# Row factors in pairs, two groups normalised on GpSimd and side rows scattered earlier, at the end of an attention and expert kernel

## The chip, the cores and the metric

One core of one Trainium2 chip. The metric is the device time of one execution in microseconds (us), the median of the runs shown. TensorE is PE in the profile, VectorE is DVE, ScalarE is ACT, GpSimd is POOL, SyncE is SP.

## What is computed

Input x is 16 x 256 rows of 256 floats. A multi-head attention layer (16 heads of 16) and a layer with 8 experts follow one another, each with a residual sum and a layer norm:

```python
x = layernorm(x + attention(x, w_q, w_k, w_v, w_o))
x = layernorm(x + experts(x, gating_w, w1, b1, w2, b2))
```

In the second, a softmax over 8 gates picks the best two experts of each of the 4,096 tokens; an expert takes at most 1,280 items, in order of tokens, and computes `relu(g @ w1 + b1) @ w2 + b2`, which is added to the token's row with its normed weight. The layer norm at the end is

```python
m = mean(x); v = var(x)
return (x - m) / sqrt(v + 1e-5)
```

## The kernel before, in words

All matrix products are made in float32 by splitting each factor into a high part and a low part (`h_hi`, `h_lo` and so on) and adding three products. ScalarE and VectorE make the parts. After attention, the rows x1 lie in DRAM twice: as the source for the experts, and as `acc_rows`, to which experts add their outputs with a scattering DMA.

The experts' part (`experts`) runs over 8 experts. An expert's 1,280 slots are 5 chunks (c = 0 to 4) of 256 rows, 2 tiles of 128 rows each, gathered by GpSimd's indirect DMAs into `rows[c]`. Layer 1 runs over "super-chunks": chunks 0 and 1, chunk 2 alone, chunks 3 and 4. A super-chunk has units: in a wide one unit u (0 to 7) is one of the 8 slices of 128 hidden features for 512 rows, six matmuls (L1685 to L1687) into one of four banks in turn. ScalarE's relu (L1475) takes a unit from its bank, VectorE splits it (L1551, L1553). TensorE waits for the relu of unit u - 4 before it fills the bank again. Layer 2 makes the chunk's output tiles (L1714 to L1716 for the last expert). The order of all of this is written out by hand in `expert_order`, and each engine runs its own part of that order.

For the last expert the end differs. Its output isn't added in DRAM. SyncE loads all 4,096 rows of `acc_rows` as eight groups of 4 x 128 rows into `acc_sb` (`a` in the code), VectorE takes their statistics (`row_stats`, L1559), GpSimd makes their row factors (`row_factors`), ScalarE normalises them (`normalise`, L1485), SyncE stores them. Rows that the last expert touches are then overwritten: GpSimd gathers the sums so far into `rows[c]` (`gather_sums`, L1377), VectorE adds the share of the last expert (L1568, L1575) and takes statistics, and when all stores have landed (`stored`) GpSimd scatters the finished rows to the output (`put_rows`, L1415).

Chunks 0 and 1 are the "side rows": GpSimd makes their factors (`fix_factors`) and ScalarE normalises them (`fixed_rows`, L1491). Chunks 2, 3 and the two tiles of chunk 4 are the "end parts" 0 to 3: VectorE makes the variance (L1593, L1600), GpSimd the factor by one power instruction (`end_factor`, L1405), VectorE normalises (`end_rows`, L1607). A factor is (variance + eps) to the power -0.5 (L1386), the column of -0.5 coming from `expo`, set by one memset.

Each engine runs its instructions in order, so a wait holds all that stands behind it. SyncE issues the eight stores in order of the groups. Groups 6 and 7 are normalised by ScalarE one tile after each relu of the last super-chunk (`IN_RELU`). Layer 2 of chunks 2 and 3 in the last expert writes to layer 1's banks, so its tiles wait for the relus of units 4, 5, 6 and 7:

```python
elif e == LASTE and c in (2, 3):
    pe.wait_ge(h_done, unit_no(e, len(SUPERS) - 1, 2 * (c - 1) + r + 2, None) + 1)
```

## Time and profile before

| what | value |
|---|---|
| time, median of 3 runs | 820.42 us (818.41 to 821.08) |
| span of the profiled execution | 856.8 us |
| TensorE matmul busy | 784.5 us, 92% |
| VectorE busy | 605.1 us, 71% |
| ScalarE busy | 442.1 us, 52% |
| GpSimd busy | 410.2 us, 48% |

The profile is of one execution; for it only the span from the first to the last instruction is given, and no second time beside it. Shares are of that span. A row of the timeline has an instruction's start, its duration, its engine and line, what it writes and reads, and in brackets the idle time of the engine before it and what ended it.

### The profile page before, as it was taken

To read this page: it belongs to the slowest core of one execution; us is meant where nothing else is said; L and a number is where in the kernel's file an instruction comes from. 1 tells how busy PE (TensorE), PEld (TensorE's weight loads), DVE (VectorE), ACT (ScalarE), POOL (GpSimd) and SP (SyncE) were. 2 spreads that over 40 slices of the span, in tenths; PEclk is the share of its full clock that TensorE was granted. 3 is DMA by queue.
4 is the path that set the end of the run, shared out by engine and by line. 5 is a ranking of instruction groups with operands and counts; after the bars stand their busy time and mean duration, and the time that the engine had idled before them with its cause. 6 is when DMAs were issued, how large, how long until landed. Compare 5 with 4: busy or idle time off the path is not lost.

```text
span 856.8 us, 16628 instructions
## 1 busy us (share of the span) xinstructions
PE 784.5 (92%) x5919; PEld 648.5 (76%) x5919; DVE 605.1 (71%) x1325; ACT 442.1 (52%) x753; POOL 410.2 (48%) x595
## 2 busy tenths in 40 slices
PE   7699989999989985896999999999999999999994
PEld 7577766677667653585889898898898888988993
DVE  5768878888888885683756856756657568665983
ACT  3166757777666664542534534534345345443670
POOL 1011245555555546457146445254364462556675
PEclk9799999999999998799899999999999999999998
DMA  5677765555555572326145245253352451533741
GB/s 158 135 165 161 161 153 113 114 113 114 116 114 110 115 141 73 116 51 180 20 91 109 41 89 115 43 130 50 81 111 40 96 112 31 140 57 57 288 179 46
DMA packets 71534, 92.75 MB, mean 108 GB/s; under 512 B 12972, under 2 KB 55885, under 8 KB 71324
## 3 DMA queue, kind: packets, MB, share of 16 engines
q1 hardware_dynamic: 53308, 67.95, 31.0%
q0 software_dynamic: 16928, 22.15, 14.9%
q10 hardware_dynamic: 1216, 1.57, 0.8%
q8 instruction: 48, 0.79, 0.4%
q14 instruction: 34, 0.28, 0.1%
HBM read 39.18 MB, written 26.89 MB: 77 GB/s over the span
## 4 chain that ended last, share of the span: by engine, by line
PE 69%; DVE 14%; issue 5%; POOL 3%; another core or an unknown queue 3%; DMA 2%; ACT 2%; ACTq 1%; POOLq 0%; DVEq 0%; SPq 0%
PE bank L1718 14%; DVE negm L890 10%; PE wide L1687 8%; PE wide L1685 8%; PE wide L1686 8%; PE bank L985 7%; PE bank L1720 7%; PE wide L1030 5%; PE bank L1664 2%; PE wide L1048 2%; PE bank L1095 2%; PE bank L1064 1%; PE bank L994 1%; POOL slot_list L533 1%
## 5 line engine op out<-in xcount | busy, mean ns | idle before, releaser
L1359 POOL DMA_INDIRECT acc_rows<-o_w,lists x70 | 120.4, 1720 | 181.6 <-ACT o_w L1508 167.9
L890 DVE TENSOR_REDUCE negm<-wide 128x4 f32<-128x1024 f32 x128 | 156.1, 1222 | 50.5 <-PE wide L1030 31.7
L630 ACT ACTIVATE probs<-wide 128x1024 f32<-128x1024 f32 x128 | 131.0, 1024 | 89.1 <-PE wide L1048 68.9
L1475 ACT ACTIVATE h<-wide,b1T 128x512 f32<-128x512 f32 (+1 forms) x200 | 115.0, 600 | 96.8 <-PE wide L1687 69.1
L1720 PE MATMUL bank<-stack,h_lo 128*128 128x256 f32 x560 | 156.9, 280 | 0.0
L1685 PE MATMUL wide<-g_hi,stack 128*128 128x512 f32 (+1 forms) x400 | 140.8, 352 | 5.2 <-DVE g_lo L1536 4.1
L1687 PE MATMUL wide<-g_hi,stack 128*128 128x512 f32 (+1 forms) x400 | 140.1, 350 | 0.1
L1686 PE MATMUL wide<-g_lo,stack 128*128 128x512 f32 (+1 forms) x400 | 140.1, 350 | 0.0
L1508 ACT ACTIVATE o_w<-o_b,lists 128x256 f32<-128x256 f32 x70 | 35.7, 510 | 148.6 <-DVE o_b L1646 135.5
L1718 PE MATMUL bank<-stack,h_hi 128*128 128x512 f32 x304 | 108.7, 401 | 1.3 <-DVE o_b L1646 1.3
L1720 PEld LDWEIGHTS bank<-stack,h_lo 128*128 128x128 f32 x560 | 105.6, 189 | 0.0
L1348 POOL DMA_INDIRECT rows<-x_rows,lists x80 | 84.3, 1054 | 29.5 <-issue 23.9
L1718 PE MATMUL bank<-stack 128*128 128x512 f32 x256 | 90.4, 396 | 0.0
L1685 PEld LDWEIGHTS wide<-g_hi,stack 128*128 128x128 f32 x400 | 75.9, 190 | 16.4 <-DVE g_lo L1536 4.4
L1030 PE MATMUL wide<-stack 48*128 48x256 f32 x512 | 65.5, 335 | 24.8 <-DVE negm L890 21.2
L1030 PEld LDWEIGHTS wide<-stack 48*128 48x128 f32 x512 | 40.2, 191 | 62.0 <-DVE negm L890 28.7
L1644 DVE TENSOR_TENSOR low<-bank,b_all 128x256 f32<-128x256 f32 x70 | 29.6, 422 | 81.4 <-PE bank L1720 69.4
L1687 PEld LDWEIGHTS wide<-g_hi,stack 128*128 128x128 f32 x400 | 75.9, 190 | 10.6 <-issue 0.3
L1686 PEld LDWEIGHTS wide<-g_lo,stack 128*128 128x128 f32 x400 | 76.0, 190 | 9.7
L1064 PE MATMUL bank<-probs,v_aug 128*32 128x256 f32 x1024 | 72.4, 402 | 9.3 <-ACT probs L630 9.3
L543 POOL CAST xT_hi<-xT_f 128x512 fp32r<-128x512 f32 x14 | 8.5, 610 | 148.3 <-ACT xT_f L585 148.3
L533 POOL DMA_INDIRECT slot_list<-item,dest x64 | 65.5, 1023 | 25.7 <-issue 23.6
(211 smaller groups left out, 1640.9 us busy)
## 6 DMA issues: line engine op xcount, KB each, us to landing
stack<-qk SPq DMA_DIRECT2D x180, 128.0 KB, 4.2
...
```

Source lines behind the costliest of these rows:

```text
L630: nc.scalar.activation(probs[:, i % 4].rearrange("p x c t -> p x (c t)"), shifted_banks(i)[:, :, :], ACT.Exp, scale=SCALE).then_inc(exp_do ...
L890: nc.vector.tensor_reduce(negm[n % 2][:, :, :, u].rearrange("p c x -> p x c"), score_banks(PAIRS * n + u)[:, :, :].rearrange("p x (c t) -> ...
L1030: ins = nc.tensor.matmul(out[:, x, c * S:c * S + S], st[k, u, 0, c * P:c * P + P], st[k, u, 1, :], start=True, stop=True, tile_position=(H ...
L1064: ins = nc.tensor.matmul(out, v_aug[n % VB][:, c, 4 * t + j, :], probs[:, u % 4, j % 2, c, :], start=(c == 0), stop=(c == QC - 1), tile_po ...
L1348: nc.gpsimd.indirect_dma_start(out=rows[c][:, r, :], out_offset=None, in_=x1_d, in_offset=bass.IndirectOffsetOnAxis(ap=lists[:, e, QC * c ...
L1359: nc.gpsimd.indirect_dma_start(out=acc_d, out_offset=bass.IndirectOffsetOnAxis(ap=lists[:, e, QC * c + r, 0:1], axis=0), in_=o_w[c][:, r, ...
L1475: ins = nc.scalar.activation(h[u % 2][:, t], banks[BZ[u % 4]][:, t], ACT.Relu, bias=b1T[:, FT * e + f:FT * e + f + 1])
L1685: nc.tensor.matmul(out, w1_hi[:, k, fs], g_hi[i % 2][:, k, cols], start=(k == 0), stop=False)
L1686: nc.tensor.matmul(out, w1_hi[:, k, fs], g_lo[i % 2][:, k, cols], start=False, stop=False)
L1687: ins = nc.tensor.matmul(out, w1_lo[:, k, fs], g_hi[i % 2][:, k, cols], start=False, stop=(k == DK - 1))
L1718: nc.tensor.matmul(banks[BO[r]], H_hi[:, f, rs], w2_both[:, f, :, :].rearrange("p x d -> p (x d)"), start=(f == 0), stop=False)
L1720: ins = nc.tensor.matmul(out_half(r, 1), H_lo[:, f, rs], w2_hi[:, f, :], start=False, stop=(f == FT - 1))
```

## The change

- `expo` grows from 4 to 8 columns.
- `row_factors` takes two groups in one set of four instructions, on 8 columns instead of 4; there are four sets where there were eight.
- GpSimd's order: the factors of groups 0 and 1, then the gathers of chunks 3 and 4 (which stood behind all factors), then the factors of groups 2 to 7.
- Groups 6 and 7 are normalised by GpSimd (`last_groups`), four tiles each, as (row - mean) x factor; they count on `own_done`, for which SyncE now waits ahead of these two stores.
- `fix_factors` makes the factors of both side chunks at once.
- The side rows' four tiles are normalised by ScalarE one after each relu of units 4 to 7 (`SIDE_UNIT`), where it had the tiles of groups 6 and 7 after all eight; before, the side rows came after the last relu.
- The four scatters of the side rows all stand before the factor of end part 0, where one stood before and three after it.

```diff
@@ -88,7 +88,7 @@
         b1T = sb("b1T", [P, NE * FT])
         w1_raw = sb("w1_raw", [P, DK, FF])
         w2_raw = sb("w2_raw", [P, FT, D])
-        expo = sb("expo", [P, 2 * QC])
+        expo = sb("expo", [P, 4 * QC])
         w1_loaded, w2_loaded, b2_loaded = sem("w1_loaded"), sem("w2_loaded"), sem("b2_loaded")
         w1_hi_done, w1_lo_done, w2_hi_done, w2_lo_done = sem("w1_hi_done"), sem("w1_lo_done"), sem("w2_hi_done"), sem("w2_lo_done")
         list0_loaded, list1_loaded, lists_loaded, late0_loaded, late_loaded = (
@@ -1203,8 +1203,9 @@
     LASTE, LASTC = NE - 1, NC - 1
     PAIR = 2
     FIRST_STATS = 2
-    IN_RELU = (6, 7)
+    OWN = (6, 7)
     SIDE = 2
+    SIDE_UNIT = 4
     LAST_BANKS = ((4, 5), (6, 7), (0, 1), (2, 3), (4, 5))
     acc_v = acc_d[0:T, :].rearrange("(g p t) d -> g p t d", p=P, t=GROUP)
     out_rows = out_d.rearrange("b s d -> (b s) d")
@@ -1253,7 +1254,7 @@
         acc_loaded = [sem(f"acc_loaded{i}") for i in range(NG)]
         stats_done, norm_parts, rstd_done, shift_done, out_done, stored = (sem(n) for n in (
             "stats2_done", "norm_parts2", "rstd2_done", "shift2_done", "out_done", "out_stored"))
-        low_done = sem("low_done")
+        low_done, own_done = sem("low_done"), sem("own_done")
         fix_stats = sb("fix_stats_sb", [P, NC, QC, 3])
         fix_veps, fix_nmean, fix_rstd, fix_shift = (sb(n, [P, NC, QC]) for n in ("fix_veps", "fix_nmean", "fix_rstd", "fix_shift"))
         end_stats = sb("end_stats", [P, QC, 6])
@@ -1332,7 +1333,10 @@
             for i in range(NG):
                 sp.dma_start(a[:, i], acc_v[i]).then_inc(acc_loaded[i], 16)
             for i in range(NG):
-                sp.wait_ge(out_done, GROUP * (i + 1))
+                if i in OWN:
+                    sp.wait_ge(own_done, GROUP * (i - OWN[0] + 1))
+                else:
+                    sp.wait_ge(out_done, GROUP * (i + 1))
                 sp.dma_start(out_v[i], a[:, i]).then_inc(stored, 16)
             sp.wait_ge(stored, 16 * NG)
             for c in range(NC):
@@ -1378,26 +1382,36 @@
                         out=rows[c][:, r, :], out_offset=None, in_=acc_d,
                         in_offset=bass.IndirectOffsetOnAxis(ap=lists[:, LASTE, QC * c + r, 0:1], axis=0)).then_inc(gathered[c], 16)
 
-            def row_factors(i):
...
+            def row_factors(b):
+                two = slice(2 * b, 2 * b + 2)
+                pool.wait_ge(stats_done, GROUP // PAIR * (2 * b + 2))
+                nc.gpsimd.tensor_scalar(veps[:, two, :], stats[:, two, :, 2], 1.0 / D, EPS, ALU.mult, ALU.add).then_inc(norm_parts, 1)
+                nc.gpsimd.tensor_scalar(nmean[:, two, :], stats[:, two, :, 1], -1.0, None, ALU.mult).then_inc(norm_parts, 1)
+                pool.wait_ge(norm_parts, 2 * b + 1)
+                nc.gpsimd.tensor_tensor(rstd[:, two, :], veps[:, two, :], minus_half[:, :].rearrange("p (i t) -> p i t", i=2),
+                                        ALU.pow).then_inc(rstd_done, 1)
+                pool.wait_ge(norm_parts, 2 * b + 2)
+                pool.wait_ge(rstd_done, b + 1)
+                nc.gpsimd.tensor_tensor(shift[:, two, :], nmean[:, two, :], rstd[:, two, :], ALU.mult).then_inc(shift_done, 1)
+
+            def last_groups():
+                pool.wait_ge(rstd_done, NG // 2)
+                for i in OWN:
+                    for t in range(GROUP):
+                        nc.gpsimd.tensor_scalar(a[:, i, t, :], a[:, i, t, :], stats[:, i, t, 1:2], rstd[:, i, t:t + 1],
+                                                ALU.subtract, ALU.mult).then_inc(own_done, 1)
+
+            def fix_factors():
+                side = slice(0, SIDE)
+                pool.wait_ge(fix_stats_done, SIDE)
+                nc.gpsimd.tensor_scalar(fix_veps[:, side, :], fix_stats[:, side, :, 2], 1.0 / D, EPS, ALU.mult, ALU.add).then_inc(norm_parts, 1)
+                nc.gpsimd.tensor_scalar(fix_nmean[:, side, :], fix_stats[:, side, :, 1], -1.0, None, ALU.mult).then_inc(norm_parts, 1)
+                pool.wait_ge(norm_parts, NG + 1)
+                nc.gpsimd.tensor_tensor(fix_rstd[:, side, :], fix_veps[:, side, :],
+                                        minus_half[:, 0:SIDE * QC].rearrange("p (c r) -> p c r", c=SIDE), ALU.pow).then_inc(rstd_done, 1)
+                pool.wait_ge(norm_parts, NG + 2)
+                pool.wait_ge(rstd_done, NG // 2 + 1)
+                nc.gpsimd.tensor_tensor(fix_shift[:, side, :], fix_nmean[:, side, :], fix_rstd[:, side, :], ALU.mult).then_inc(shift_done, 1)
 
             def end_factor(j):
                 c, cols = END_PARTS[j]
@@ -1409,7 +1423,7 @@
 
                 for r in tiles:
                     if c < SIDE:
-                        pool.wait_ge(out_done, GROUP * NG + QC * c + r + 1)
+                        pool.wait_ge(out_done, GROUP * OWN[0] + QC * c + r + 1)
                     else:
                         pool.wait_ge(fix_out_done, QC * (c - SIDE) + r + 1)
                     nc.gpsimd.indirect_dma_start(
@@ -1422,19 +1436,17 @@
                 add_back(n // NC, n % NC)
             for c in range(3):
                 gather_sums(c)
-            for i in range(FIRST_STATS):
-                row_factors(i)
-            for i in range(FIRST_STATS, NG):
-                row_factors(i)
+            row_factors(0)
             gather_sums(3)
             gather_sums(4)
+            for b in range(1, NG // 2):
+                row_factors(b)
+            last_groups()
+            fix_factors()
+            pool.wait_ge(stored, 16 * NG)
             for c in range(SIDE):
-                fix_factors(c)
-            pool.wait_ge(stored, 16 * NG)
-            put_rows(0, (0,))
+                put_rows(c)
             end_factor(0)
-            put_rows(0, (1,))
-            put_rows(1)
             put_rows(2)
             end_factor(1)
             put_rows(3)
@@ -1475,31 +1487,26 @@
                         ins = nc.scalar.activation(h[u % 2][:, t], banks[BZ[u % 4]][:, t], ACT.Relu,
                                                    bias=b1T[:, FT * e + f:FT * e + f + 1])
                     ins.then_inc(h_done, 1)
-                    if e == LASTE and s == len(SUPERS) - 1:
-                        i, t = divmod(u, GROUP)
-                        normalise(IN_RELU[i], (t,))
-
-            def normalise(i, tiles=range(GROUP)):
-                act.wait_ge(shift_done, i + 1)
-                for t in tiles:
+                    if e == LASTE and s == len(SUPERS) - 1 and u >= SIDE_UNIT:
+                        fixed_row(*divmod(u - SIDE_UNIT, QC))
+
+            def normalise(i):
+                act.wait_ge(shift_done, i // 2 + 1)
+                for t in range(GROUP):
                     nc.scalar.activation(a[:, i, t, :], a[:, i, t, :], ACT.Identity, bias=shift[:, i, t:t + 1],
                                          scale=rstd[:, i, t:t + 1]).then_inc(out_done, 1)
 
-            def fixed_rows(c):
-                act.wait_ge(shift_done, NG + c + 1)
-                for r in range(QC):
-                    nc.scalar.activation(rows[c][:, r, :], rows[c][:, r, :], ACT.Identity, bias=fix_shift[:, c, r:r + 1],
-                                         scale=fix_rstd[:, c, r:r + 1]).then_inc(out_done, 1)
+            def fixed_row(c, r):
+                act.wait_ge(shift_done, NG // 2 + 1)
+                nc.scalar.activation(rows[c][:, r, :], rows[c][:, r, :], ACT.Identity, bias=fix_shift[:, c, r:r + 1],
+                                     scale=fix_rstd[:, c, r:r + 1]).then_inc(out_done, 1)
 
             def weigh(e, c, tiles=range(QC)):
                 n = NC * e + c
                 if e == LASTE:
                     if c == 0:
-                        for i in range(IN_RELU[0]):
+                        for i in range(OWN[0]):
                             normalise(i)
-                    if c == 2:
-                        for i in range(SIDE):
-                            fixed_rows(i)
                     return
                 if e > 0:
                     act.wait_ge(added[c], 16 * QC * e)
@@ -1601,7 +1608,7 @@
 
             def end_rows(j):
                 c, cols = END_PARTS[j]
-                dve.wait_ge(rstd_done, NG + SIDE + j + 1)
+                dve.wait_ge(rstd_done, NG // 2 + 1 + j + 1)
                 for r in range(cols.start, cols.stop):
                     mean = fix_stats[:, c, r, 1:2] if c < LASTC else end_mv[:, r, 0:1]
                     nc.vector.tensor_scalar(rows[c][:, r, :], rows[c][:, r, :], mean, fix_rstd[:, c, r:r + 1],
```

GpSimd from the last three rows of the first gathers on, before:

```order
L1377 DMA rows<-acc_rows,lists 128x256 [waits added2,added3,added1,added4,added0,gT_ready]
L1377 DMA rows<-acc_rows,lists 128x256
L1383 TENSOR_SCALAR veps<-stats 128x4 [waits stats2_done]
L1384 TENSOR_SCALAR nmean<-stats 128x4
L1386 TENSOR_TENSOR rstd<-veps,expo 128x4 [waits norm_parts2]
L1389 TENSOR_TENSOR shift<-nmean,rstd 128x4 [waits rstd2_done,norm_parts2]
L1383 TENSOR_SCALAR veps<-stats 128x4 [waits stats2_done]
L1384 TENSOR_SCALAR nmean<-stats 128x4
L1386 TENSOR_TENSOR rstd<-veps,expo 128x4 [waits norm_parts2]
L1389 TENSOR_TENSOR shift<-nmean,rstd 128x4 [waits rstd2_done,norm_parts2]
L1383 TENSOR_SCALAR veps<-stats 128x4 [waits stats2_done]
L1384 TENSOR_SCALAR nmean<-stats 128x4
L1386 TENSOR_TENSOR rstd<-veps,expo 128x4 [waits norm_parts2]
L1389 TENSOR_TENSOR shift<-nmean,rstd 128x4 [waits rstd2_done,norm_parts2]
```

and now:

```order
L1381 DMA rows<-acc_rows,lists 128x256 [waits added2,added3,added1,added4,added0,gT_ready]
L1381 DMA rows<-acc_rows,lists 128x256
L1388 TENSOR_SCALAR veps<-stats 128x8 [waits stats2_done]
L1389 TENSOR_SCALAR nmean<-stats 128x8
L1391 TENSOR_TENSOR rstd<-veps,expo 128x8 [waits norm_parts2]
L1395 TENSOR_TENSOR shift<-nmean,rstd 128x8 [waits rstd2_done,norm_parts2]
L1381 DMA rows<-acc_rows,lists 128x256 [waits added2,added3,added1,added4,added0,gT_ready]
L1381 DMA rows<-acc_rows,lists 128x256
L1381 DMA rows<-acc_rows,lists 128x256 [waits added2,added3,added1,added4,added0,gT_ready]
L1381 DMA rows<-acc_rows,lists 128x256
L1388 TENSOR_SCALAR veps<-stats 128x8 [waits stats2_done]
L1389 TENSOR_SCALAR nmean<-stats 128x8
L1391 TENSOR_TENSOR rstd<-veps,expo 128x8 [waits norm_parts2]
L1395 TENSOR_TENSOR shift<-nmean,rstd 128x8 [waits rstd2_done,norm_parts2]
L1388 TENSOR_SCALAR veps<-stats 128x8 [waits stats2_done]
L1389 TENSOR_SCALAR nmean<-stats 128x8
L1391 TENSOR_TENSOR rstd<-veps,expo 128x8 [waits norm_parts2]
L1395 TENSOR_TENSOR shift<-nmean,rstd 128x8 [waits rstd2_done,norm_parts2]
L1388 TENSOR_SCALAR veps<-stats 128x8 [waits stats2_done]
L1389 TENSOR_SCALAR nmean<-stats 128x8
L1391 TENSOR_TENSOR rstd<-veps,expo 128x8 [waits norm_parts2]
L1395 TENSOR_TENSOR shift<-nmean,rstd 128x8 [waits rstd2_done,norm_parts2]
L1401 TENSOR_SCALAR acc_sb<-acc_sb,stats,rstd 128x256 [waits rstd2_done]
L1401 TENSOR_SCALAR acc_sb<-acc_sb,stats,rstd 128x256 x7
L1407 TENSOR_SCALAR fix_veps<-fix_stats_sb 128x4 [waits fix_stats_done]
```

The factors of groups 2 to 7 have gone behind the gathers of chunks 3 and 4, three sets of four instructions instead of six, and the eight tiles of `acc_sb` stand between the last of them and the side factors.

GpSimd at its end, before:

```order
L1415 DMA out<-rows,lists 4096x256 [waits out_done,out_stored]
L1405 TENSOR_TENSOR fix_rstd<-fix_veps,expo 128x2 [waits end_steps]
L1415 DMA out<-rows,lists 4096x256 [waits out_done] x3
L1415 DMA out<-rows,lists 4096x256 [waits fix_out_done] x2
L1405 TENSOR_TENSOR fix_rstd<-fix_veps,expo 128x2 [waits end_steps]
L1415 DMA out<-rows,lists 4096x256 [waits fix_out_done] x2
L1405 TENSOR_TENSOR fix_rstd<-fix_veps,expo 128x1 [waits end_steps]
L1415 DMA out<-rows,lists 4096x256 [waits fix_out_done]
L1405 TENSOR_TENSOR fix_rstd<-fix_veps,expo 128x1 [waits end_steps]
L1415 DMA out<-rows,lists 4096x256 [waits fix_out_done]
```

and now:

```order
L1414 TENSOR_TENSOR fix_shift<-fix_nmean,fix_rstd 128x4 [waits rstd2_done,norm_parts2]
L1429 DMA out<-rows,lists 4096x256 [waits out_done,out_stored]
L1429 DMA out<-rows,lists 4096x256 [waits out_done] x3
L1419 TENSOR_TENSOR fix_rstd<-fix_veps,expo 128x2 [waits end_steps]
L1429 DMA out<-rows,lists 4096x256 [waits fix_out_done] x2
L1419 TENSOR_TENSOR fix_rstd<-fix_veps,expo 128x2 [waits end_steps]
L1429 DMA out<-rows,lists 4096x256 [waits fix_out_done] x2
L1419 TENSOR_TENSOR fix_rstd<-fix_veps,expo 128x1 [waits end_steps]
L1429 DMA out<-rows,lists 4096x256 [waits fix_out_done]
L1419 TENSOR_TENSOR fix_rstd<-fix_veps,expo 128x1 [waits end_steps]
L1429 DMA out<-rows,lists 4096x256 [waits fix_out_done]
```

The three scatters of side rows that stood behind the first factor of an end part (L1405, now L1419) now stand ahead of it.

ScalarE at its end now, from the last normalised group on (the relus are L1487):

```order
L1496 ACTIVATE acc_sb<-acc_sb,shift,rstd 128x256 [waits shift2_done]
L1496 ACTIVATE acc_sb<-acc_sb,shift,rstd 128x256 x3
L1487 ACTIVATE h<-wide,b1T 128x512 [waits h_lo_done,z_ready,h_hi_done] x5
L1501 ACTIVATE rows<-rows,fix_shift,fix_rstd 128x256 [waits shift2_done]
L1487 ACTIVATE h<-wide,b1T 128x512 [waits h_lo_done,z_ready,h_hi_done]
L1501 ACTIVATE rows<-rows,fix_shift,fix_rstd 128x256 [waits shift2_done]
L1487 ACTIVATE h<-wide,b1T 128x512 [waits h_lo_done,z_ready,h_hi_done]
L1501 ACTIVATE rows<-rows,fix_shift,fix_rstd 128x256 [waits shift2_done]
L1487 ACTIVATE h<-wide,b1T 128x512 [waits h_lo_done,z_ready,h_hi_done]
L1501 ACTIVATE rows<-rows,fix_shift,fix_rstd 128x256 [waits shift2_done]
```

Before, each of the eight relus had one tile of `acc_sb` behind it, and the four tiles of side rows stood after the last.

## Rows read from the trace of the kernel before

**Rows 1.** The page: the chain that ended last, shares by engine.

```profile
PE 69%; DVE 14%; issue 5%; POOL 3%; another core or an unknown queue 3%; DMA 2%; ACT 2%; ACTq 1%; POOLq 0%; DVEq 0%; SPq 0%
```

**Rows 2.** Two stretches: busy us (x instructions) by engine, TensorE's clock, DMA.

```profile
806.00:840.00 34.00, 34.00 (x242) 31.90 (x241) 29.62 (x59) 23.71 (x46) 25.94 (x46) 1.00 0.49 187
840.00:850.00 10.00, 4.05 (x34) 3.84 (x33) 3.81 (x12) 0.00 (x0) 6.43 (x8) 0.93 0.16 54
```

**Rows 3.** Timeline of GpSimd in the tail.

```profile
834.27 0.88 POOL L1405 TENSOR_TENSOR fix_rstd<-fix_veps,expo 128x2 f32<-128x2 f32 x1 [0.78 <-DVE fix_veps L1593]
...
840.80 0.97 POOL L1415 DMA_INDIRECT out<-rows,lists  x1 [0.30 <-issue]
841.78 0.74 POOL L1405 TENSOR_TENSOR fix_rstd<-fix_veps,expo 128x2 f32<-128x2 f32 x1
843.78 1.04 POOL L1415 DMA_INDIRECT out<-rows,lists  x1 [1.26 <-DVE rows L1607]
...
846.11 0.60 POOL L1405 TENSOR_TENSOR fix_rstd<-fix_veps,expo 128x1 f32<-128x1 f32 x1
...
850.87 1.04 POOL L1415 DMA_INDIRECT out<-rows,lists  x1 [1.26 <-DVE rows L1607]
```

**Rows 4.** Timeline of VectorE: splits of the last super-chunk, then the tail.

```profile
820.56 0.40 DVE L1551 CAST stack<-h 128x512 fp32r<-128x512 f32 x1
...
828.84 0.69 DVE L1553 TENSOR_TENSOR h_lo<-h,stack 128x512 fp32r<-128x512 f32 x1
...
839.73 0.17 DVE L1593 TENSOR_SCALAR fix_veps<-fix_stats_sb 128x2 f32<-128x2 f32 x1
...
842.56 0.74 DVE L1607 TENSOR_SCALAR rows<-rows,fix_stats_sb,fix_rstd 128x256 f32<-128x256 f32 x2 [2.66 <-POOL fix_rstd L1405]
...
847.06 0.48 DVE L1575 SCALAR_TENSOR_TENSOR rows<-bank,lists,rows 128x256 f32<-128x256 f32 x1
```

**Rows 5.** Timeline of TensorE: first matmul of unit 4, of layer 2, and the last.

```profile
821.12 0.39 PE L1685 MATMUL wide<-g_hi,stack 128*128 128x512 f32 x1
...
826.69 0.28 PE L1714 MATMUL wide<-stack,h_hi 128*128 128x256 f32 x1
...
843.77 0.28 PE L1716 MATMUL bank<-stack,h_lo 128*128 128x256 f32 x1
```

**Rows 6.** Timeline of ScalarE: groups 0 to 5, then the first relu.

```profile
806.67 4.05 ACT L1485 ACTIVATE acc_sb<-acc_sb,shift,rstd 128x256 f32<-128x256 f32 x8
811.56 6.02 ACT L1485 ACTIVATE acc_sb<-acc_sb,shift,rstd 128x256 f32<-128x256 f32 x12 [0.84 <-POOL shift L1389]
817.79 2.08 ACT L1485 ACTIVATE acc_sb<-acc_sb,shift,rstd 128x256 f32<-128x256 f32 x4 [0.21 <-POOL shift L1389]
819.77 0.67 ACT L1475 ACTIVATE h<-wide,b1T 128x512 f32<-128x512 f32 x1
```

**Rows 7.** Timeline of GpSimd: factors, gathers, and one disturbed instruction.

```profile
803.80 1.18 POOL L1386 TENSOR_TENSOR rstd<-veps,expo 128x4 f32<-128x4 f32 x1
...
811.61 0.20 POOL L1383 TENSOR_SCALAR veps<-stats 128x4 f32<-128x4 f32 x1
...
812.08 1.04 POOL L1386 TENSOR_TENSOR rstd<-veps,expo 128x4 f32<-128x4 f32 x1
813.26 0.20 POOL L1389 TENSOR_TENSOR shift<-nmean,rstd 128x4 f32<-128x4 f32 x1
...
822.44 1.26 POOL L1377 DMA_INDIRECT rows<-acc_rows,lists  x1 [0.69 <-issue]
...
826.55 0.95 POOL L1377 DMA_INDIRECT rows<-acc_rows,lists  x1 [0.30 <-issue]
...
827.86 0.98 POOL L1395 TENSOR_SCALAR fix_nmean<-fix_stats_sb 128x2 f32<-128x2 f32 x1
```

**Rows 8.** Groups of GpSimd by shape: busy, mean ns, idle before.

```profile
L547 POOL TENSOR_TENSOR xT_lo<-xT_f,xT_hi 128x512 fp32r<-128x512 f32 x14 | 17.9, 1279 | 1.2
...
L543 POOL CAST xT_hi<-xT_f 128x512 fp32r<-128x512 f32 x14 | 8.5, 610 | 148.3 <-ACT xT_f L585 148.3
```

More of the change, by code:

```diff
@@ L1379, in gather_sums @@
                         in_offset=bass.IndirectOffsetOnAxis(ap=lists[:, LASTE, QC * c + r, 0:1], axis=0)).then_inc(gathered[c], 16)
-            def row_factors(i):
-                pool.wait_ge(stats_done, GROUP // PAIR * (i + 1))
-                nc.gpsimd.tensor_scalar(veps[:, i, :], stats[:, i, :, 2], 1.0 / D, EPS, ALU.mult, ALU.add).then_inc(norm_parts, 1)
-                nc.gpsimd.tensor_scalar(nmean[:, i, :], stats[:, i, :, 1], -1.0, None, ALU.mult).then_inc(norm_parts, 1)
-                pool.wait_ge(norm_parts, 2 * i + 1)
-                nc.gpsimd.tensor_tensor(rstd[:, i, :], veps[:, i, :], minus_half[:, :], ALU.pow).then_inc(rstd_done, 1)
-                pool.wait_ge(norm_parts, 2 * i + 2)
-                pool.wait_ge(rstd_done, i + 1)
-                nc.gpsimd.tensor_tensor(shift[:, i, :], nmean[:, i, :], rstd[:, i, :], ALU.mult).then_inc(shift_done, 1)
@@ L1391, in fix_factors @@
-            def fix_factors(c):
-                j = NG + c
-                pool.wait_ge(fix_stats_done, c + 1)
-                nc.gpsimd.tensor_scalar(fix_veps[:, c, :], fix_stats[:, c, :, 2], 1.0 / D, EPS, ALU.mult, ALU.add).then_inc(norm_parts, 1)
-                nc.gpsimd.tensor_scalar(fix_nmean[:, c, :], fix_stats[:, c, :, 1], -1.0, None, ALU.mult).then_inc(norm_parts, 1)
-                pool.wait_ge(norm_parts, 2 * j + 1)
-                nc.gpsimd.tensor_tensor(fix_rstd[:, c, :], fix_veps[:, c, :], minus_half[:, 0:QC], ALU.pow).then_inc(rstd_done, 1)
-                pool.wait_ge(norm_parts, 2 * j + 2)
-                pool.wait_ge(rstd_done, j + 1)
-                nc.gpsimd.tensor_tensor(fix_shift[:, c, :], fix_nmean[:, c, :], fix_rstd[:, c, :], ALU.mult).then_inc(shift_done, 1)
+            def row_factors(b):
[9 more added lines that the diff above has]
+                nc.gpsimd.tensor_tensor(shift[:, two, :], nmean[:, two, :], rstd[:, two, :], ALU.mult).then_inc(shift_done, 1)
```

## The prediction

> **What bounds the kernel now.** I read the page first: TensorE is the largest share of the chain that ended last, but VectorE (14%) and GpSimd (3%) stand on it too, and the change touches only the end [rows 1]. So I read the end by stages: TensorE is busy without a gap to 840 and stops inside 840 to 845, yet the span goes on to 856.8 [rows 2]. Two parts of the end decide, and everything below is told in the times of that one execution.
>
> *The tail, from 832 on.* GpSimd's rows show scatter DMAs (L1415) one each 1.27 us (0.97 and 0.30 of issue), of the four side tiles and of chunk 2's two, the last starting at 840.80, and the row factor of chunk 3 (L1405) only behind them at 841.78 [rows 3]. What it needs, the variance of chunk 3, was ready at 839.73 + 0.17 = 839.90 [rows 4]: so GpSimd's queue was late by 841.78 - 839.95 = 1.83 us. From there the work alternates: factor, VectorE normalises (L1607, it waited 2.66 us for the factor), scatter, next factor. The last scatter starts at 850.87, 9.09 us after 841.78 [rows 3, 4]. TensorE was done at 843.77 + 0.28 = 844.05 [rows 5], before VectorE asked for its last sum at 847.06 [rows 4]. The tail is bound by GpSimd's order, not by TensorE.
>
> *The stage before, 806 to 828.* ScalarE normalises groups 0 to 5 (8 + 12 + 4 instructions, 0.50 us each), then starts the relu of unit 0 of the last super-chunk at 819.77, done at 820.44 [rows 6]. TensorE starts unit 4 (which takes unit 0's bank) at 821.12, with no gap [rows 5]. So ScalarE has 0.68 us to spare, and beyond that each us that it is late holds TensorE, and with it everything behind.
>
> **The change part by part.**
>
> 1. *Side rows ahead.* The four scatters of chunks 0 and 1 now stand before the factor of chunk 2. If they are issued before chunk 2's variance is there (the factor starts at 834.27, released by it [rows 3]), only chunk 2's own two are left before chunk 3's factor. Chunk 2's scatters then run 836.9 to 839.2 (VectorE's first row of chunk 2 at about 836.1, plus 0.81, the distance from a normalised tile at 842.97 to the scatter at 843.78; then 1.27 and 0.97 [rows 3, 4]). Chunk 3's factor starts at 839.95 as soon as its variance is there, and the 9.09 us behind it are the same instructions as before. TensorE's 844.05 still comes before VectorE's last sum (845.2). **Tail: -1.83 us.**
>
> 2. *Factors for two groups at once, and the gathers of chunks 3 and 4 (four DMAs) moved ahead of groups 2 to 7.* The power instruction costs 0.60, 0.74 and 1.04 us for 1, 2 and 4 columns [rows 3, 7], some 0.15 a column, so I take 1.64 for 8: 0.6 more than one of 4. The trace has none of 8. From below it is 1.04 (nothing more than for 4), from above 2.08 (twice that); I take the line through the three rows. For groups 0 and 1: power at 803.80 now 1.18 + 0.6, shift done at 806.0; ScalarE asks at 806.67, so it costs nothing there [rows 6, 7]. Next stand the gathers: 0.69 of issue and 5.06 us for four (822.44 to 827.50) [rows 7], so 806.0 to 811.8. They don't wait: chunks 3 and 4 are transposed by then, since ScalarE converts them before it turns to the groups at 806.67 [rows 6]. Then groups 2 and 3: a group took 1.85 us (811.61 to 813.26 + 0.20) [rows 7], two now 2.45, done at 814.3. Before, ScalarE had group 2 at 811.56 [rows 6]. **ScalarE starts group 2 some 2.7 us later.** Groups 4 and 5 are ready at 816.9 and no longer in the way. 16 instructions (12 took 6.02, 4 took 2.08) end at 814.3 + 8.05 = 822.35, the relu of unit 0 starts 0.1 before that as it did before, ends at 822.9, and TensorE takes unit 4 at 823.05, the 0.12 between them being what lay between that relu's end and VectorE's split at 820.56 [rows 4]. Against 821.12 that is a hold of **+1.92 us**. With the bounds of the power (it counts twice, -0.6 or +0.44 each) the hold is 0.7 to 2.8 us. Nothing takes it back: TensorE has no gap from there to its end [rows 2]. All times of the tail move with it, and part 1's gain stays what it is.
>
> 3. *GpSimd normalises groups 6 and 7.* Eight instructions leave ScalarE's relus, eight of 128x256 come to GpSimd. For units 0 to 3 ScalarE has nothing between relus; they are held by VectorE's splits, so it gains nothing on TensorE. On GpSimd the nearest rows are the one-input cast of 128x512 (0.61) and the two-input subtract of 128x512 (1.28) [rows 8]; half of each is 0.31 and 0.64, and the bounds are 0.31 and the whole 1.28. I take p = 0.5, near the cast, as there is one tensor read. Factors of groups 6 and 7 end at 819.4, the eight at 823.4, the side factors (four columns: 1.85 as for a group, and 0.6 if VectorE disturbs them as it did the instruction at 827.86 [rows 7]) at 825.9. ScalarE wants them after the relu of unit 4, about 827.0 (relus keep pace with VectorE's splits, 0.40 + 0.69 a unit [rows 4], from 823.05): covered by 1.1 us. If p grows, the cover is gone at 0.64, but TensorE feels it only when the relu of unit 5 is later than 831.5, where layer 2 of chunk 2, second tile, waits for it (layer 2 began at 826.69 and made six tiles by 843.9, 2.87 each [rows 5]: 826.69 + 1.92 + 2.87); that needs the side shift by 830.3, so p up to about **1.07**. Behind a late shift stand on ScalarE the relus of units 5, 6 and 7. Cost: 0.
>
> 4. *Stores and scatters.* SyncE now waits for group 5 at 822.4 and group 7 at 823.4, where before group 7's last tile stood behind the last relu; so the wait for all stores that stands ahead of the scatters ends earlier. The scatters follow the four side rows (827.5 to 830.7) with 0.8 us and end at about 833.1; chunk 2's factor could start at 834.27 + 1.92 = 836.2. Slack 3 us: cost 0. The queues' earlier gathers meet loads that are nearly over; VectorE's statistics hide them, so I give that nothing. Fewer GpSimd instructions (18 less) count only in the times above.
>
> **Sum:** -1.83 + 1.92 = +0.1 us, so the span 856.8 becomes 856.9. The profiled execution's span stands 36.4 us above the median of the runs shown (820.42), and no row says where; I carry the difference over in full: **820.5 us**. About 0.3% (2.5 us) is what a measurement of this kernel can tell from no change.
>
> **Rivals.**
>
> *The gain alone.* If 8 columns cost the power what 4 do, and ScalarE runs a little tighter, the hold is 0.7 or less and the result lies between -1.1 and -1.83: 818.6 to 819.3. For it: TensorE's slack of 0.68 us, and timed runs that are 4% shorter than this trace, so that the gathers may be too. Against it: the four gathers alone delay group 2 by more than the slack. Chance 0.23.
>
> *GpSimd too slow for the eight tiles, so that the relus stall.* Place: the side shift on ScalarE between the relus of units 4 and 5. It decides from p = 1.07, and each us of p above costs 8 us. At p = 1.28 it is 8 x 0.21 = +1.7 (822.2). While VectorE ran its casts and two-input subtracts, GpSimd's tensor-scalar on two columns took 0.98, against 0.20 for one on four columns undisturbed [rows 7]; if each of the eight also waits for one VectorE subtract of 0.69 [rows 4], p = 1.28 + 0.69 = 1.97 and it costs +7.2 (827.7). For it: those rows, and no row of this instruction. Against it: VectorE has little to do from 820.6 to 823.0, when most of the eight run, and its statistics before that left GpSimd undisturbed (0.20, while they ran). Chance 0.14. The Trainium skill, SBUF — State Buffer, section "SBUF: two separate sides", says that VectorE in a two-port mode or with two SBUF inputs and GpSimd take a shared port pair as an exclusive lock, and the loser blocks for the whole instruction. By that rule alone, 0.69 on each of the eight, p is 1.19 and the sum 1.0 us more, 821.5; the 0.98 agrees with it, the 0.20 says that it doesn't always strike.
>
> *The side rows don't get out of the way.* If stores or side rows come so late that their scatters still stand before chunk 3's factor, the gain is lost and the hold stays: 820.4 + 1.9 = 822.3. It would need the side rows 6 us later than I have them. Chance 0.06.
>
> **How the numbers follow.** My case has 0.57, the rivals 0.23, 0.14 and 0.06. My case with its bounds spans 819.3 to 821.4; the first rival reaches down to 818.6, the third and the lower part of the second up to 822.3. With the scatter of the medians (818.41 to 821.08) the range is 818.4 to 822.7, which leaves out the dear half of the second rival and the best luck. Faster by over 0.3% takes the first rival and some 0.7 us more: 0.12. Slower by over 0.3% takes the second rival with p above 1.38, or the third and some luck: 0.16. Within: 0.72.
>
> **What would show it.** In the profile after: chunk 3's factor directly behind its variance, with GpSimd idle before it, and the last scatter 9.1 us later; side scatters done before chunk 2's factor. A gap of near 1.9 us on TensorE before unit 4, released by the relu, and ScalarE's group 2 starting near 814.3. The power on 8 columns near 1.64. The eight tiles on GpSimd near 0.5. Wrong it would be if that gap on TensorE is under 0.7, if the power isn't in the 1.04 to 2.08, or if ScalarE waits for the side shift by more than 3 us.

## The result, and the profile after

| kernel | median us (range, runs) | ratio to before, 95% interval |
|---|---|---|
| before | 820.84 (818.41 to 821.79, 7) | |
| changed | 823.95 (821.89 to 826.25, 7) | 1.0036 [1.0022, 1.0051] |

The change made the kernel 3.1 us slower. The forecast was 820.5 us with a range to 822.7.

The profiled execution of the changed kernel has a span of 822.4 us in a run of 824.11 us, so some 1.7 us lie around the span. The profile before (856.8) was held up far ahead of the end, in places that the change doesn't touch. Matched instruction by instruction on TensorE, it falls behind the profile after by some 16 us up to 329, by 13 more up to 365 (in the stretch 330 to 350 TensorE's clock was 0.83 and 0.50, and TensorE was busy 2.43 us of the first ten) and by the rest up to 444; from there to the last super-chunk the distance stays at 37.5. What held it up is not shown. So spans aren't compared; the end is, from TensorE's first matmul of the last super-chunk to the start of the last scatter. That is 850.87 - 815.55 = 35.32 us before and 816.46 - 778.02 = 38.44 us after: **3.12 us more**, all of the difference (3.1 us) between the medians. What stood at 815.55 before stands 37.5 earlier now.

TensorE's timeline, its first matmul of the last super-chunk and the two that waited in the end:

```profile
778.02 0.39 PE L1692 MATMUL wide<-g_hi,stack 128*128 128x512 f32 x1
...
785.70 0.50 PE L1692 MATMUL wide<-g_hi,stack 128*128 128x512 f32 x1 [1.94 <-ACT h L1487]
...
795.94 0.39 PE L1721 MATMUL wide<-stack,h_hi 128*128 128x256 f32 x1 [1.54 <-ACT h L1487]
```

The first gap is the hold that was forecast, in its place, at unit 4: [rows 5] had none. From the first matmul of unit 0 to that of unit 4 it is 785.70 - 778.02 = 7.68 us, and 821.12 - 815.55 = 5.57 before: a hold of 2.11, where 1.92 was forecast (the 1.94 in the row is idle time alone). The second, 1.54 us at the second tile of chunk 2, was part of a rival. ScalarE shows what made both:

```profile
777.09 7.99 ACT L1496 ACTIVATE acc_sb<-acc_sb,shift,rstd 128x256 f32<-128x256 f32 x16 [3.68 <-POOL shift L1395]
784.99 1.24 ACT L1487 ACTIVATE h<-wide,b1T 128x512 f32<-128x512 f32 x2
...
794.72 0.60 ACT L1501 ACTIVATE rows<-rows,fix_shift,fix_rstd 128x256 f32<-128x256 f32 x1 [3.97 <-POOL fix_shift L1414]
795.22 0.67 ACT L1487 ACTIVATE h<-wide,b1T 128x512 f32<-128x512 f32 x1
```

Groups 2 to 5 begin 3.68 us after ScalarE was free, and [rows 6] answers to that with 0.84. The side rows (L1501) waited 3.97 us for GpSimd's side shift, with the relu of unit 5 behind them. GpSimd, from the power on eight columns on:

```profile
775.02 1.69 POOL L1391 TENSOR_TENSOR rstd<-veps,expo 128x8 f32<-128x8 f32 x1
...
782.22 10.51 POOL L1401 TENSOR_SCALAR acc_sb<-acc_sb,stats,rstd 128x256 f32<-128x256 f32 x8
...
794.48 0.20 POOL L1414 TENSOR_TENSOR fix_shift<-fix_nmean,fix_rstd 128x4 f32<-128x4 f32 x1
796.26 1.11 POOL L1429 DMA_INDIRECT out<-rows,lists  x1 [1.57 <-DMA out<-acc_sb]
...
800.23 1.09 POOL L1429 DMA_INDIRECT out<-rows,lists  x1 [0.30 <-issue]
802.42 0.88 POOL L1419 TENSOR_TENSOR fix_rstd<-fix_veps,expo 128x2 f32<-128x2 f32 x1 [1.10 <-DVE fix_veps L1600]
...
807.37 0.74 POOL L1419 TENSOR_TENSOR fix_rstd<-fix_veps,expo 128x2 f32<-128x2 f32 x1
...
816.46 1.04 POOL L1429 DMA_INDIRECT out<-rows,lists  x1 [1.26 <-DVE rows L1614]
```

The eight tiles of groups 6 and 7 (L1401) take 782.22 to 792.8, 1.32 us each on average: the first three, before VectorE's splits, 1.22 from start to start, the other five 1.39. So the side shift is there only at 794.68. The side scatters are out of the way before chunk 2's factor (802.42), but that factor comes 24.4 us after the super-chunk's start, where it came 834.27 - 815.55 = 18.7 after it in [rows 3]. VectorE lies between the side shift and that factor:

```profile
785.68 0.48 DVE L1558 CAST stack<-h 128x512 fp32r<-128x512 f32 x1 [2.52 <-ACT h L1487]
786.20 0.93 DVE L1560 TENSOR_TENSOR h_lo<-h,stack 128x512 fp32r<-128x512 f32 x1
...
795.92 0.43 DVE L1558 CAST stack<-h 128x512 fp32r<-128x512 f32 x1 [3.33 <-ACT h L1487]
...
798.93 0.75 DVE L1560 TENSOR_TENSOR h_lo<-h,stack 128x512 fp32r<-128x512 f32 x1
...
802.17 0.17 DVE L1600 TENSOR_SCALAR fix_veps<-fix_stats_sb 128x2 f32<-128x2 f32 x1
...
806.25 0.17 DVE L1600 TENSOR_SCALAR fix_veps<-fix_stats_sb 128x2 f32<-128x2 f32 x1
...
808.15 0.73 DVE L1614 TENSOR_SCALAR rows<-rows,fix_stats_sb,fix_rstd 128x256 f32<-128x256 f32 x2 [1.73 <-POOL fix_rstd L1419]
```

It splits units 5 to 7 only from 795.92 on, then takes the sums and the variance of chunk 2 (802.17). [rows 4] had the splits of a unit at 0.40 and 0.69, here 0.48 and 0.93 while GpSimd's tiles ran. Chunk 3's variance was ready at 806.42, and its factor came at 807.37, behind the second scatter of chunk 2: still 0.95 us late. So the forecast sign of a factor directly behind its variance did not show in this kernel.

### The profile page after: what moved, and what is told of

The parts are those of the page before. It is cut to its first block, busy times and chain, and to the rows that moved or that the text cites. A ratio compares the mean times of both kernels' runs of the same rounds, so it can differ in the third digit from the quotient of the medians.

```text
span 822.4 us, 16603 instructions
## 1 busy us (share of the span) xinstructions
PE 772.8 (94%) x5919; PEld 643.3 (78%) x5919; DVE 606.3 (74%) x1325; ACT 438.8 (53%) x745; POOL 411.7 (50%) x583
## 3 DMA queue, kind: packets, MB, share of 16 engines
q10 hardware_dynamic: 1216, 1.57, 0.9%
## 4 chain that ended last, share of the span: by engine, by line
PE 69%; DVE 13%; POOL 8%; issue 5%; DMA 3%; ACT 1%; ACTq 1%; POOLq 0%; SPq 0%; DVEq 0%
PE bank L1725 14%; PE bank L985 11%; DVE negm L890 9%; PE wide L1694 7%; PE wide L1693 7%; PE wide L1692 7%; PE bank L1727 7%; PE wide L1030 7%; PE wide L1048 2%; PE bank L994 2%; PE bank L1671 2%; PE bank L1095 1%; POOL acc_sb L1401 1%; POOL slot_list L533 1%; DMA acc_rows<-o_w,lists 1%
## 5 line engine op out<-in xcount | busy, mean ns | idle before, releaser
L1487 ACT ACTIVATE h<-wide,b1T 128x512 f32<-128x512 f32 (+1 forms) x200 | 115.2, 601 | 92.6 <-PE wide L1694 66.5
L1515 ACT ACTIVATE o_w<-o_b,lists 128x256 f32<-128x256 f32 x70 | 35.7, 510 | 148.3 <-DVE o_b L1653 148.3
L1692 PEld LDWEIGHTS wide<-g_hi,stack 128*128 128x128 f32 x400 | 75.4, 189 | 13.9 <-ACT h L1487 3.2
L1064 PE MATMUL bank<-probs,v_aug 128*32 128x256 f32 x1024 | 68.5, 385 | 1.0 <-ACT probs L630 1.0
```

What stands on the lines that cost most here:

```text
L1487: ins = nc.scalar.activation(h[u % 2][:, t], banks[BZ[u % 4]][:, t], ACT.Relu, bias=b1T[:, FT * e + f:FT * e + f + 1])
L1692: nc.tensor.matmul(out, w1_hi[:, k, fs], g_hi[i % 2][:, k, cols], start=(k == 0), stop=False)
```

## The experiments

Each was run beside the kernel before. "End" is the stretch defined above, in the profile of each, less the 35.32 us of before.

| label | what | ratio, 95% interval | end, us |
|---|---|---|---|
| changed | | 1.0036 [1.0022, 1.0051] | +3.12 |
| e1_small_tiles | tiles of 8 columns | 1.0005 [0.9994, 1.0016] | +0.39 |
| e2_small_late_gathers | and gathers behind the factors | 1.0024 [1.0011, 1.0037] | +2.32 |
| e3_factors_first | side factors ahead of the tiles | 1.0057 [1.0036, 1.0078] | +5.08 |
| e4_tiles_on_vector | tiles on VectorE | 1.0004 [0.9993, 1.0014] | +0.16 |
| e5_forms | other forms among the eight | one run | +0.75 |
| e9_columns | fewer columns in three of the eight | one run | +0.96 |
| e6_small_gathers_last | e1, gathers behind side factors | 0.9985 [0.9975, 0.9995] | -0.90 |
| e7_vector_one_group | whole, rearranged | 0.9984 [0.9970, 0.9998] | -1.70 |
| e8_and_factors_early | e7, and the last factors earlier | 0.9957 [0.9943, 0.9971] | -2.66 |

**e1_small_tiles.** The price of the tiles taken away, their place kept.

```diff
-    nc.gpsimd.tensor_scalar(a[:, i, t, :], a[:, i, t, :], stats[:, i, t, 1:2], rstd[:, i, t:t + 1],
+    nc.gpsimd.tensor_scalar(a[:, i, t, 0:8], a[:, i, t, 0:8], stats[:, i, t, 1:2], rstd[:, i, t:t + 1],
```

> The changed kernel, but GpSimd's eight instructions on groups 6 and 7 take 8 of 256 columns (the other 248 columns of those tiles are left out of the normalisation). Theory A (the price p = 1.37 us of these eight is what made the change slower): ScalarE gets the side shift about 9.4 us earlier and no longer waits for it, TensorE's second gap (1.5 us at layer 2 of chunk 2) is gone, the first (1.9 us at unit 4) stays, chunk 3's factor stands directly behind its variance; 0.1 us above the kernel before, ratio 1.000. Rival B (the new order of the side scatters and the gathers is slow by itself): still 3 us slower, ratio 1.004.

It came as theory A had it, 1.0005. GpSimd's timeline:

```profile
780.59 3.07 POOL L1401 TENSOR_SCALAR acc_sb<-acc_sb,stats,rstd 128x8 f32<-128x8 f32 x8
...
785.75 0.60 POOL L1414 TENSOR_TENSOR fix_shift<-fix_nmean,fix_rstd 128x4 f32<-128x4 f32 x1
...
797.31 0.89 POOL L1419 TENSOR_TENSOR fix_rstd<-fix_veps,expo 128x2 f32<-128x2 f32 x1 [1.96 <-DVE fix_veps L1600]
...
803.03 0.72 POOL L1419 TENSOR_TENSOR fix_rstd<-fix_veps,expo 128x2 f32<-128x2 f32 x1 [0.79 <-DVE fix_veps L1600]
...
812.10 1.04 POOL L1429 DMA_INDIRECT out<-rows,lists  x1 [1.25 <-DVE rows L1614]
```

The side shift comes at 786.35, and chunk 3's factor (803.03) follows a wait for its variance, not a scatter. TensorE's waits in this stretch (us, times, longest):

```profile
PE wide L1692 <- ACT h L1487: 1.9, 1, 1.9
```

That is one wait, the first. So all but 0.4 us of the loss hung on the price of the eight tiles; what is left is hold less gain, 2.11 less 1.7, forecast at +0.1.

**e2_small_late_gathers.** Meant to take away TensorE's first gap.

```diff
-            row_factors(0)
+            for b in range(NG // 2):
+                row_factors(b)
             gather_sums(3)
             gather_sums(4)
-            for b in range(1, NG // 2):
-                row_factors(b)
```

> As the kernel with small tiles (248 columns of each tile of groups 6 and 7 are left out of the normalisation), and the gathers of chunks 3 and 4 behind all four sets of row factors instead of behind the first. Theory A: ScalarE has group 2 some 2.5 us earlier, TensorE's gap at unit 4 is gone, the tail keeps its 1.8 us: 1.8 us faster than the kernel before, ratio 0.998. Rival C (TensorE's gap at unit 4 doesn't matter, since the tail is bound by GpSimd's chain): the same time as with small tiles alone.

Both missed: 1.0024. The first gap shrank to 0.7, but the four gathers now stood ahead of the tiles and the side factors. GpSimd's tiles of 8 columns and ScalarE's first side row:

```profile
786.86 4.87 POOL L1401 TENSOR_SCALAR acc_sb<-acc_sb,stats,rstd 128x8 f32<-128x8 f32 x8
```

```profile
793.74 0.60 ACT L1500 ACTIVATE rows<-rows,fix_shift,fix_rstd 128x256 f32<-128x256 f32 x1 [5.03 <-POOL fix_shift L1414]
```

ScalarE waited 5.03 us, and the old stall was back by another way. It tells something all the same: from the side shift to the last scatter it is 815.59 - 793.70 = 21.9 us here and 816.46 - 794.68 = 21.8 in the changed kernel. Once the side shift is late, the end hangs on it alone in these two traces, whatever gap TensorE had at unit 4 (0.66 here, 1.94 in the changed kernel).

**e3_factors_first.** Does only ScalarE's wait cost?

```diff
-            last_groups()
             fix_factors()
+            last_groups()
```

> The changed kernel with the side factors ahead of the eight tiles on GpSimd. Theory A: ScalarE no longer waits for the side shift and TensorE's second gap is gone, but the eight tiles (11 us) end 2.9 us later, the last store lands later, and the four side scatters (5 us) start only behind it and stand in front of chunk 2's factor: chunk 3's factor is late again, some 1 us later than in the changed kernel; 4 us above the kernel before, ratio 1.005. Rival D (only the wait of ScalarE costs): as the kernel before, ratio 1.000.

Theory A holds (1.0057), D doesn't. TensorE's second gap is gone, but the last store is later:

```profile
785.89 11.25 POOL L1401 TENSOR_SCALAR acc_sb<-acc_sb,stats,rstd 128x256 f32<-128x256 f32 x8
800.66 1.11 POOL L1429 DMA_INDIRECT out<-rows,lists  x1 [3.52 <-DMA out<-acc_sb]
...
805.79 0.74 POOL L1419 TENSOR_TENSOR fix_rstd<-fix_veps,expo 128x2 f32<-128x2 f32 x1
...
819.21 1.04 POOL L1429 DMA_INDIRECT out<-rows,lists  x1 [1.26 <-DVE rows L1614]
```

The tiles end at 797.1 and the side scatters wait 3.52 us for the store behind them, then stand in front of chunk 2's factor.

**e4_tiles_on_vector.** The same eight tiles, whole, on VectorE behind the side sums.

```diff
+            def last_groups():
+                dve.wait_ge(rstd_done, NG // 2)
+                for i in OWN:
+                    for t in range(GROUP):
+                        nc.vector.tensor_scalar(a[:, i, t, :], a[:, i, t, :], stats[:, i, t, 1:2], rstd[:, i, t:t + 1],
+                                                ALU.subtract, ALU.mult).then_inc(own_done, 1)
...
                         fixed_sums(i)
+                    last_groups()
```

> The changed kernel with the eight tiles of groups 6 and 7 on VectorE, behind the sums of the side rows, where the changed kernel's trace has VectorE idle for 2.5 us. At 0.37 us a tile (two took 0.73 at the end) they are 2.9 us, so the split of unit 0 is 0.4 us late and nothing waits for it. Theory A: no wait for the side shift, one gap of 1.9 us on TensorE; 0.1 to 0.5 us above the kernel before, ratio 1.000 to 1.001. Rival B: still 3 us slower.

1.0004, as theory A. VectorE's row of the eight:

```profile
782.02 2.65 DVE L1613 TENSOR_SCALAR acc_sb<-acc_sb,stats,rstd 128x256 f32<-128x256 f32 x8
```

0.33 us a tile where GpSimd took 1.22 to 1.39; the first split came at 784.60, after which nothing was late.

**e5_forms and e9_columns.** The price itself, in one run each. In e5 the eight have different forms (two constants; one operation with the mean; a copy; 128 and 64 columns; a product); in e9 the first three have 128, 64 and 8 columns and the fourth is one operation with a constant:

```diff
+                        cols = {0: 128, 1: 64, 2: 8}.get(k, D)
+                        at = a[:, i, t, 0:cols]
+                        if k == 3:
+                            ins = nc.gpsimd.tensor_scalar(at, at, 0.5, None, ALU.subtract)
+                        else:
+                            ins = nc.gpsimd.tensor_scalar(at, at, m, r, ALU.subtract, ALU.mult)
```

> The changed kernel with five different instructions among the eight of GpSimd on groups 6 and 7 (the values of those two groups aren't normalised as they should be): in order, the form as it was; two constants instead of the mean and the factor of the row; one operation with the row's mean; a copy; the form as it was on 128 columns and on 64 columns; a product of the tile with itself; the form as it was. This measures the price by form. Theory E (the two values per row, read from memory, make it dear): constants 0.45 us, one operation with the mean about 0.8, 128 and 64 columns 0.8 and 0.5, copy 0.4, product 0.75, whole form 1.25 to 1.38. Theory F (two operations make it dear, whatever the operands): constants 1.2, one operation 0.7.

> The changed kernel with other instructions among GpSimd's eight on groups 6 and 7 (whose values aren't normalised as they should be): first the form as it was on 128, 64 and 8 columns, then one operation with a constant on 256, then four as they were. The first four run before VectorE's splits begin, so this gives the price by columns undisturbed; in the kernel with five forms the 128 and the 64 columns (1.06 and 0.91 us) ran beside VectorE's splits. Theory H (a fixed part of 0.35 us and 3.5 ns a column): 128 columns 0.80, 64 columns 0.57, 8 columns 0.38. Theory I (the fixed part is 0.8 us or more): 128 and 64 columns as before, 1.06 and 0.91. One operation with a constant: 0.7 to 0.93.

GpSimd's groups by form in e5 (busy, mean ns), then rows of its timeline in e9:

```profile
L1417 POOL TENSOR_SCALAR acc_sb<-acc_sb,stats,rstd 128x256 f32<-128x256 f32 x2 | 2.6, 1316 | 0.0
L1405 POOL TENSOR_SCALAR acc_sb<-acc_sb 128x256 f32<-128x256 f32 x1 | 1.1, 1077 | 0.0
...
L1407 POOL TENSOR_SCALAR acc_sb<-acc_sb,stats 128x256 f32<-128x256 f32 x1 | 0.9, 925 | 0.0
...
L1409 POOL CAST acc_sb<-acc_sb 128x256 fp32r<-128x256 f32 x1 | 0.4, 397 | 0.0
```

```profile
782.09 0.81 POOL L1409 TENSOR_SCALAR acc_sb<-acc_sb,stats,rstd 128x128 f32<-128x128 f32 x1
...
783.45 0.40 POOL L1409 TENSOR_SCALAR acc_sb<-acc_sb,stats,rstd 128x8 f32<-128x8 f32 x1
783.83 0.87 POOL L1407 TENSOR_SCALAR acc_sb<-acc_sb 128x256 f32<-128x256 f32 x1
784.67 1.23 POOL L1409 TENSOR_SCALAR acc_sb<-acc_sb,stats,rstd 128x256 f32<-128x256 f32 x1
...
787.25 1.38 POOL L1409 TENSOR_SCALAR acc_sb<-acc_sb,stats,rstd 128x256 f32<-128x256 f32 x1
```

Undisturbed, the form with mean and factor costs 0.40 on 8 columns, 0.81 on 128 and 1.23 on 256: a fixed 0.38 us and 3.3 ns a column, close to theory H (0.35 and 3.5). Neither E nor F holds alone: two constants still cost 1.08, one constant 0.87, one operation with the mean 0.93, and a copy 0.40. The largest step, 0.47, lies between the copy (in e5 a cast to another float32 form) and one operation with a constant; a second operation adds 0.21, and reading the row's two values 0.15. The Trainium skill, GPSIMD Engine Reference, section "4.1 Engine selection", has GpSimd about twice as slow as VectorE for two inputs and calls one input roughly line-rate. VectorE took 0.33 for the whole form, so the copy's 0.40 is near that, and the tensor-scalar's 0.87 to 1.23 on the same 256 columns is not.

e5 and e9 show one thing more. Their eight instructions are cheaper together, and TensorE had a single gap again, the one at unit 4; ScalarE still waited 1.86 us for the side shift. From e5, TensorE's waits in the end, then GpSimd, ScalarE and the last scatter:

```profile
PE wide L1708 <- ACT h L1503: 1.8, 1, 1.8
```

```profile
793.41 0.20 POOL L1430 TENSOR_TENSOR fix_shift<-fix_nmean,fix_rstd 128x4 f32<-128x4 f32 x1
793.65 0.60 ACT L1517 ACTIVATE rows<-rows,fix_shift,fix_rstd 128x256 f32<-128x256 f32 x1 [1.86 <-POOL fix_shift L1430]
...
815.38 1.04 POOL L1445 DMA_INDIRECT out<-rows,lists  x1 [1.26 <-DVE rows L1630]
```

The last scatter comes 815.38 - 793.61 = 21.8 us after the side shift, as in the changed kernel and in e2, and 21.8 in e9. The end is 0.75 and 0.96 us over before, where e1 has 0.39. So a late side shift costs even where TensorE doesn't wait for the relu of unit 5.

**e6_small_gathers_last.** The question of e2 again, with the gathers behind the side factors too.

```diff
-            row_factors(0)
-            gather_sums(3)
-            gather_sums(4)
-            for b in range(1, NG // 2):
+            for b in range(NG // 2):
                 row_factors(b)
             last_groups()
             fix_factors()
+            gather_sums(3)
+            gather_sums(4)
```

> As the kernel with small tiles (248 columns of each tile of groups 6 and 7 are left out of the normalisation), and the gathers of chunks 3 and 4 behind the side factors. The kernel with small tiles and late gathers didn't test TensorE's gap at unit 4 alone, since its side shift came 5 us late; here it comes in time. Theory A: TensorE's gap at unit 4 shrinks from 1.9 to 0.7 us (GpSimd still waits for the statistics of group 3), the tail keeps its gain: 1.1 us faster than the kernel before, ratio 0.9986. Rival C (that gap is worth nothing at the end): ratio 1.0005, as with small tiles alone.

0.9985. TensorE's only wait in the end:

```profile
PE wide L1691 <- ACT h L1486: 0.7, 1, 0.7
```

Unit 4 comes 6.41 us after unit 0 where e1 has 7.68, so the hold is 1.27 us smaller, and the end is 1.29 us shorter than in e1: TensorE's first gap reaches the end in full, as long as the side shift is in time. The 0.7 that stays isn't the gathers' but the pairing's: GpSimd waits for group 3's statistics before it makes group 2's factors.

```profile
775.30 0.20 POOL L1388 TENSOR_SCALAR veps<-stats 128x8 f32<-128x8 f32 x1 [4.75 <-DVE stats L1565]
```

**e7_vector_one_group.** Group 7 on VectorE, group 6 with the relus, factors of groups 2 and 3 singly.

```diff
-    OWN = (6, 7)
+    OWN = (7,)
+    FACTOR_SETS = ((0, 1), (2,), (3,), (4, 5), (6, 7))
...
             row_factors(0)
             gather_sums(3)
+            for k in range(1, SETS):
+                row_factors(k)
             gather_sums(4)
```

> The changed kernel, whole, arranged by what the runs showed: VectorE normalises group 7 (four tiles, 1.5 us) behind the side sums, ScalarE group 6 in the relus of units 0 to 3, factors in sets of groups (0, 1), 2, 3, (4, 5), (6, 7), the gathers of chunk 3 behind the first set (where GpSimd waits for statistics) and those of chunk 4 behind the last. Theory A: no gap on TensorE, side shift in time, side scatters ahead of chunk 2's factor: only the tail's gain is left, 1.8 us faster than the kernel before, ratio 0.998. Rival B (moving the side scatters gains nothing, whatever stands before): ratio 1.000 or above.

TensorE has no wait in the end, and the ratio is 0.9984, the end 1.70 us shorter. Chunk 3's variance and its factor in this trace, where the super-chunk starts at 778.48:

```profile
802.78 0.17 DVE L1600 TENSOR_SCALAR fix_veps<-fix_stats_sb 128x2 f32<-128x2 f32 x1
```

```profile
803.03 0.72 POOL L1418 TENSOR_TENSOR fix_rstd<-fix_veps,expo 128x2 f32<-128x2 f32 x1 [0.79 <-DVE fix_veps L1600]
```

The variance is ready 24.47 us after the start (24.35 before) and the factor starts at 24.55, where it was 26.23 before. So the gain is that of a factor that no longer stands behind scatters, forecast at 1.83.

**e8_and_factors_early.** The tail's own order.

```diff
-            put_rows(3)
+            put_rows(3, (0,))
             end_factor(2)
-            put_rows(LASTC, (0,))
+            put_rows(3, (1,))
             end_factor(3)
-            put_rows(LASTC, (1,))
+            put_rows(LASTC)
```

> As the kernel with one group on VectorE, and at the very end on GpSimd the factor of chunk 4's first tile stands between the two scatters of chunk 3, that of its second tile ahead of both scatters of chunk 4. Theory A (the tail is GpSimd's chain of scatters and factors): each factor is as early as its variance, the last scatter starts 1.4 us earlier still; 3.2 us faster than the kernel before, ratio 0.996. Rival G (the last tiles are bound by TensorE's end and VectorE's sums): as without it, ratio 0.998.

```profile
805.51 1.04 POOL L1428 DMA_INDIRECT out<-rows,lists  x1 [1.26 <-DVE rows L1614]
806.58 0.59 POOL L1418 TENSOR_TENSOR fix_rstd<-fix_veps,expo 128x1 f32<-128x1 f32 x1
807.36 1.05 POOL L1428 DMA_INDIRECT out<-rows,lists  x1 [0.19 <-issue]
809.13 0.57 POOL L1418 TENSOR_TENSOR fix_rstd<-fix_veps,expo 128x1 f32<-128x1 f32 x1 [0.73 <-DVE fix_veps L1607]
809.89 1.16 POOL L1428 DMA_INDIRECT out<-rows,lists  x1 [0.19 <-issue]
811.36 0.97 POOL L1428 DMA_INDIRECT out<-rows,lists  x1 [0.31 <-issue]
```

The factor of chunk 4's first tile starts at 806.58 where it had stood behind one more scatter, and that of the second waits only for its variance (809.13). 0.9957, from 6 runs: 3.5 us faster than before, the best of all. The last scatter is 2.66 us earlier against before in the trace, inside the interval of the timed runs (2.4 to 4.7 us), and 0.96 earlier than in e7 by that measure, where 1.4 was expected: behind the last factor two scatters now follow each other, and the second starts 1.47 after the first.

## Why the prediction was wrong, by its own steps

1. *Side rows ahead, -1.83.* Right where the side shift is in time: e7 has -1.70 in the trace, 0.9984. In the changed kernel itself the gain was not to be had, since chunk 2's variance came late and chunk 3's factor stood behind chunk 2's scatters again.
2. *Pairs and gathers, a hold of 1.92.* Right: 2.11 in the trace. The power on eight columns took 1.69 (forecast 1.64). e6 shows that the hold counts in full, but in the changed kernel the late side shift covered it.
3. *GpSimd's tiles at p = 0.5 and cost 0.* **This is the step that failed.** I had no row of the instruction and put it near the cast, because there is one tensor read. It costs 1.23 undisturbed and 1.38 beside VectorE's splits, 1.32 over the eight. The upper bound I had named, 1.28, was the nearer one. The mechanism stood in the text as a rival with a chance of 0.14, at 8 us for each us of p above 1.07. By that rule 1.32 gives +2.0, and with the other two +2.1 or 822.5, still inside the range, where +3.1 was measured. (The text's own times, 830.3 less 825.9 over eight tiles, give 1.05 for the limit.) e1 and e4 show that the price is the cause: take it away, by columns or by engine, and all but 0.4 and 0.2 us of the loss is gone. Of the three signs of being wrong that I had named, the one that came is this step's: ScalarE waited 3.97 us for the side shift.

The missing 1.0 us has mostly to do with a second path that the rival didn't have, so step 3 failed in its path too. I let the relu of unit 5 reach TensorE only. The chain of the changed kernel goes from the side shift over the relu of unit 5 to VectorE's splits of units 5, 6 and 7, its sums, chunk 2's variance (802.34) and only then to GpSimd's tail. VectorE makes the three splits ahead of the sums, so the whole of the late relus falls on chunk 2's variance. In e1 the last scatter comes 812.10 - 776.39 = 35.7 us after the super-chunk's start; with 21.8 us from the shift on, the shift may be at most 13.9 us after it. In the changed kernel that is 791.9, or a p of 0.98, not 1.07. From there to the 1.32 it is 2.8 us, and e1's 0.4 makes it the 3.1 that was measured. e5 and e9, with the shift 14.3 and 14.5 us after the start and no second gap on TensorE, lie on the same line.

4. *Stores and scatters, 0.* Right in the changed kernel (GpSimd has 12 instructions less, not the 18 of the text, which nothing hung on), though the stores' wait became visible (1.57 us ahead of the first scatter), and e3 shows how it bites: move the tiles behind the side factors, and the last store decides.

The rule on the shared port was weighed as a rival with 1.0 us. What the runs show is smaller and has two sides: a tile on GpSimd 1.23 to 1.38, VectorE's two splits of a unit from 1.09 to 1.41 busy. By the Trainium skill, SBUF — State Buffer, section "SBUF: two separate sides", whoever starts first gets the pair for the whole instruction and the other fully blocks. A subtract of 0.69 and a tile of 1.23 one after the other would take 1.92, and the trace has one of each in every 1.4 us: by these records they overlap for the greater part.
